# Sampled score maxima turned by VectorE in 32x32 blocks and stacked by 16 small DMAs a unit, in a 16-head attention layer

## The reference

```python
xn = _layernorm(x, axis=-1)
q = _split_heads(xn @ q_w.T + q_b, h) / scale        # k and v likewise
scores = jnp.einsum('bhqd,bhkd->bhqk', q, k)
attn = jax.nn.softmax(scores.astype(jnp.float32), axis=-1)
ctx = jnp.einsum('bhqk,bhkd->bhqd', attn, v)
x = x + (ctx @ out_w.T + out_b) + ffn(xn)             # ffn: fp8-rounded x and weight, 256 x 256
```

## Time and profile before

| what | us |
|---|---|
| median of 3 runs | 1987.59 (1986.44 to 1989.02) |
| the profiled execution, its own time | 1988.86 |
| its span (first to last instruction) | 1987.0 |
| PE busy | 1932.5 |
| ACT busy | 1827.5 |
| DVE busy | 1277.2 |

### The profile page before, as it was taken

How to read it: one execution, slowest core, us unless ns; L and a number is a source line. 1 busy time by engine, 2 the same in 40 slices (tenths; PEclk the granted TensorE clock), 3 DMA queues, 4 the chain that set the end, 5 groups by cost and what they waited for, 6 DMA issues and landing times.

```text
span 1987.0 us, 39086 instructions
## 1 busy us (share of the span) xinstructions
PE 1932.5 (97%) x13433; PEld 652.1 (33%) x13433; DVE 1277.2 (64%) x1789; ACT 1827.5 (92%) x2004; POOL 43.9 (2%) x53
## 2 busy tenths in 40 slices
PE   5969999999999999999999999999999999999988
PEld 3623333333333333333333333333333333333327
DVE  6645766656566766656566766656565766656556
ACT  2339999999999999999999999999999999999983
POOL 2000000000000000000000000000000000000000
PEclk9979999999999999999999999999999999999999
DMA  6870121203030121203030121202030121102022
GB/s 196 268 245 6 21 29 24 30 8 45 8 41 12 17 29 24 29 8 45 8 44 9 16 29 24 30 13 41 8 45 8 16 29 24 30 17 37 8 41 86
DMA packets 65524, 82.10 MB, mean 41 GB/s; under 512 B 9952, under 2 KB 47360, under 8 KB 62208
## 3 DMA queue, kind: packets, MB, share of 16 engines
q1 hardware_dynamic: 65472, 81.58, 20.3%
HBM read 54.79 MB, written 26.21 MB: 41 GB/s over the span
## 4 chain that ended last, share of the span: by engine, by line
PE 95%; DMA 2%; SPq 1%; DVE 1%; issue 1%; ACT 0%; ACTq 0%; DVEq 0%
PE banks L1086 48%; PE banks L1065 38%; PE banks L1092 3%; PE banks L976 2%; PE banks L1192 1%; PE banks L987 1%; DMA k_parts<-probs 1%; PE banks L1023 1%; PE banks L1043 0%; PE banks L1176 0%; PE banks L1183 0%; PE banks L960 0%; DMA q_st<-q_parts 0%; SPq L339 0%; DMA k_parts<-bits 0%
## 5 line engine op out<-in xcount | busy, mean ns | idle before, releaser
L583 ACT ACTIVATE probs<-banks 128x1024 f32<-128x1024 f32 x1923 | 1776.9, 1165 | 21.5 <-PE banks L1065 12.9
L1086 PE MATMUL banks<-probs,v_st 128*32 128x512 f32 x7680 | 1027.1, 607 | 2.9 <-DVE o_sb L800 2.9
L1065 PE MATMUL banks<-q_st,k_st 50*128 50x512 f32 x4102 | 833.2, 462 | 6.6 <-ACT probs L583 4.3
L1065 PEld LDWEIGHTS banks<-q_st,k_st 50*128 50x128 f32 x4102 | 373.7, 184 | 882.7 <-ACT probs L583 854.4
L834 DVE SCALAR_TENSOR_TENSOR d_probs<-d_probs,bits 128x1024 f32<-128x1024 f32 x256 | 313.7, 1225 | 8.8
L819 DVE TENSOR_SCALAR bits<-banks 128x512 int32<-128x512 f32 x256 | 177.2, 692 | 171.9 <-PE banks L1065 159.7
L1086 PEld LDWEIGHTS banks<-probs,v_st 128*32 128x32 f32 x7680 | 151.7, 108 | 305.3 <-issue 243.3
L800 DVE STREAM_TRANSPOSE o_sb<-banks 128x512 f32<-128x512 f32 x32 | 22.9, 717 | 299.7 <-PE banks L1086 299.7
L830 DVE SCALAR_TENSOR_TENSOR d_probs<-bits 128x1024 f32<-128x1024 f32 x128 | 156.9, 1226 | 7.3
L837 DVE SCALAR_TENSOR_TENSOR d_probs<-d_probs,powers 128x1024 f32<-128x1024 f32 x128 | 158.0, 1234 | 4.4
L825 DVE TENSOR_SCALAR bits<-bits 128x1024 int32<-128x1024 int32 x128 | 88.9, 695 | 4.4
(11 more groups left out here) (91 smaller groups left out, 482.9 us busy)
## 6 DMA issues: line engine op xcount, KB each, us to landing
k_st<-k_parts SPq DMA_DIRECT2D x204, 128.0 KB, 4.4
q_st<-q_parts SPq DMA_DIRECT2D x204, 64.0 KB, 5.0
q_parts<-probs SPq DMA_DIRECT2D x9, 512.0 KB, 6.1
k_parts<-probs SPq DMA_DIRECT2D x9, 512.0 KB, 6.2
xnT_copy<-probs SPq DMA_DIRECT2D x8, 512.0 KB, 4.4
probs<-xnT_copy SPq DMA_DIRECT2D x8, 512.0 KB, 6.7
w_f<-xnT_copy SPq DMA_DIRECT2D x16, 256.0 KB, 5.1
out_dram<-qt SPq DMA_DIRECT2D x16, 256.0 KB, 2.1
```

The costliest lines, as they stand in the source:

```text
L583: act.activation(probs[:, at:at + WIDE * CHUNK].rearrange("p (t c) -> p t c", t=WIDE), banks[:, bank:bank + WIDE, :], ACT.Exp, scale=1.0 / ...
L1065: return pe.matmul(out, k_mm[rows, kt * P:(kt + 1) * P], blocks[rows, qb // GROUPS], start=True, stop=True)
L1086: last = pe.matmul(banks[VCOLS * qb:VCOLS * (qb + 1), 6, :], v_st[:, kt, :], probs[:, at:at + CHUNK], start=first_one, stop=last_one, tile ...
```

## The change

The transposition on TensorE and its place in the order of jobs (slot 46; chunk 5 in the prologue) go, and with them the copy out of `misc` and the semaphore between VectorE and TensorE. VectorE makes the remainder part in rounded form, waits for it, and transposes `neg`, now 128x32, into `neg_row`, now 128x32 as well. Its transposition works on blocks of 32x32: row 32b + c of `neg_row` then holds column c of `neg` for the queries 32b to 32b + 31. A row of q's stack must therefore be put together from four blocks: `load_rows` issues 2 parts x 2 groups x 4 blocks = 16 DMAs a unit, each of 8 pieces of 32 values, in place of 4. The order of SyncE's queue stays. In the prologue VectorE does the whole at the start of chunk 5.

```diff
-    ROW_LOADS = 16 * GROUPS * PARTS
+    BLOCKS = P // (PARTS * UT)
+    ROW_LOADS = 16 * GROUPS * PARTS * BLOCKS
...
-        neg = sb("neg", [P, P // UT, UT])
+        neg = sb("neg", [P, PARTS, UT])
-        neg_row = sb("neg_row", [PARTS * UT, P])
+        neg_row = sb("neg_row", [P, PARTS * UT])
...
                 sp.wait_ge(c.row_ready, count)
                 for i in range(PARTS):
                     for g in range(GROUPS):
-                        at = g * GROUP + KROWS + i
-                        sp.dma_start(q_st[at:at + 1, u * UG:(u + 1) * UG].rearrange("o (t c) -> o t c", c=P),
-                                     neg_row[i * UT + g * GT:i * UT + (g + 1) * GT, :]).then_inc(c.row_in[u], 16)
+                        at, r0 = g * GROUP + KROWS + i, i * UT + g * GT
+                        to = q_st[at:at + 1, u * UG:(u + 1) * UG].rearrange("o (t b x) -> o b t x", t=GT, x=PARTS * UT)
+                        for b in range(BLOCKS):
+                            first_row = b * PARTS * UT + r0
+                            sp.dma_start(to[:, b], neg_row[first_row:first_row + GT, :]).then_inc(c.row_in[u], 16)
...
-                def minus_maxima(job, link0):
-                    negate(link0)
-                    to_rows(job)
...
-                    dve.tensor_tensor(neg[:, 1, :], neg_full[:, :], neg[:, 0, :], ALU.subtract).then_inc(c.neg_ready, 1)
-
-                def to_rows(job):
-                    dve.wait_ge(c.misc_full, job + 1)
-                    dve.tensor_copy(neg_row[:, :].bitcast(F32R), misc[0:PARTS * UT, 0:P]
-                                    ).then_inc(c.row_ready, 1)
-                    dve.wait_ge(c.row_ready, neg_count[0])
-                    dve.sem_inc(c.misc_free, 1)
+                    chain(dve.tensor_tensor(neg[:, 1, :].bitcast(F32R), neg_full[:, :], neg[:, 0, :], ALU.subtract),
+                          link0 + 3)
+                    dve.transpose(neg_row[:, :], neg[:, :, :].rearrange("p a t -> p (a t)")).then_inc(c.row_ready, 1)
...
-                def turn_maxima(job, count):
-                    misc_job(job, True)
-                    pe.wait_ge(c.neg_ready, count)
-                    pe.transpose(misc[:, 0:P], neg[:, :, :].rearrange("p a t -> p (a t)"), ident[:, :]).then_inc(c.misc_full, 1)
...
-                        if n == TURN_FIRST:
-                            turn_maxima(c.max_jobs, 1)
...
-                            jobs[u * UE + MAX_TURN] = (
-                                lambda u=u: turn_maxima(job_of[u] + (D_JOBS + c.max_jobs), h * 2 + (2 + u)))
```

More of the change, by code:

```diff
@@ L81, in program @@
     HALF = 2 * CHUNK
-    MAX_SLOTS, MAX_TURN = (36, 38), 46
+    MAX_SLOTS = (36, 38)
     UT4 = QB * len(A_ROWS)
@@ L224, in __init__ @@
                 self.misc_free = sem(f"{tag}_misc_free")
-                self.neg_ready = sem(f"{tag}_neg_ready")
                 self.row_ready = sem(f"{tag}_row_ready")
@@ L232, in __init__ @@
                 self.max_jobs = UT * (S // CHUNK) if full else 1
-                self.unit_jobs = QB * len(D_ROWS) + self.max_jobs + 1
+                self.unit_jobs = QB * len(D_ROWS) + self.max_jobs
                 self.head_jobs = UNITS * self.unit_jobs
@@ L746, in attend @@
             def attend(c):
-                MAX_LINKS = 2 + c.full * UT
+                MAX_LINKS = 3 + c.full * UT
                 SUM_LINKS = 2 if c.full else 3
@@ L769, in maxima @@
                         dve.wait_ge(c.misc_free, job0 + c.max_jobs)
-                    minus_maxima(job0 + c.max_jobs, link0)
+                    minus_maxima(link0)
                 def some_maxima(job):
@@ L776, in some_maxima, with minus_maxima @@
                                       ).then_inc(c.misc_free, 1)
-                def minus_maxima(job, link0):
-                    negate(link0)
-                    to_rows(job)
-                def negate(link0):
+                def minus_maxima(link0):
                     above = 0.0 if c.full else HEADROOM * UNIT
@@ L786, in negate @@
                     chain(dve.tensor_copy(neg[:, 0, :].bitcast(F32R), neg_full[:, :]), link0 + 2)
-                    dve.tensor_tensor(neg[:, 1, :], neg_full[:, :], neg[:, 0, :], ALU.subtract).then_inc(c.neg_ready, 1)
-                def to_rows(job):
-                    dve.wait_ge(c.misc_full, job + 1)
-                    dve.tensor_copy(neg_row[:, :].bitcast(F32R), misc[0:PARTS * UT, 0:P]
-                                    ).then_inc(c.row_ready, 1)
-                    dve.wait_ge(c.row_ready, neg_count[0])
-                    dve.sem_inc(c.misc_free, 1)
-                neg_count = [1]
+                    chain(dve.tensor_tensor(neg[:, 1, :].bitcast(F32R), neg_full[:, :], neg[:, 0, :], ALU.subtract),
+                          link0 + 3)
+                    dve.transpose(neg_row[:, :], neg[:, :, :].rearrange("p a t -> p (a t)")).then_inc(c.row_ready, 1)
                 def take_sums(h, u, link0):
@@ L855, in attend @@
                             dve.wait_ge(c.misc_free, c.max_jobs)
-                            negate(0)
+                            minus_maxima(0)
                         remainders(NCH + n, n % 2, 1, (0,))
-                        if n == TURN_FIRST:
-                            to_rows(c.max_jobs)
                         remainders(NCH + n, n % 2, 1, (1,))
@@ L874, in attend @@
                     maxima(0, 0)
-                JOB0 = c.max_jobs + 1
+                JOB0 = c.max_jobs
                 with dve.Fori(0, HEADS) as h:
@@ L878, in attend @@
                     lk = h * HEAD_LINKS + MAX_LINKS
-                    neg_count[0] = h * 2 + 2
                     for d in range(len(D_ROWS)):
@@ L889, in attend @@
                             d_exponentials(h, 1, d, half, job + (QB * d + 2 * half))
-                    neg_count[0] = h * 2 + 3
                     lk = lk + (MAX_LINKS + SUM_LINKS)
@@ L920, in _ @@
                 attend(second)
-                dve.wait_ge(second.misc_free, HEADS * second.head_jobs + second.max_jobs + 1)
+                dve.wait_ge(second.misc_free, HEADS * second.head_jobs + second.max_jobs)
                 dve.sem_inc(pass2_end, 1)
@@ L1098, in attend @@
                     all_max_jobs(0, 0, LOADS, True)
-                    pe.wait_ge(c.misc_free, c.max_jobs)
-                    turn_maxima(c.max_jobs, 1)
                 else:
@@ L1140, in maximum_first @@
                         all_max_jobs(u, j0, h * LOADS + LOADS * (1 + nxt))
-                        turn_maxima(j0 + c.max_jobs, h * 2 + (2 if u else 3))
                     for e in range(HE):
@@ L1157, in _ @@
             attend(first)
-            pe.wait_ge(first.misc_free, HEADS * first.head_jobs + first.max_jobs + 1)
+            pe.wait_ge(first.misc_free, HEADS * first.head_jobs + first.max_jobs)
             pe.wait_ge(flag_ok, 1)
@@ L1164, in _ @@
                 attend(second)
-                pe.wait_ge(second.misc_free, HEADS * second.head_jobs + second.max_jobs + 1)
+                pe.wait_ge(second.misc_free, HEADS * second.head_jobs + second.max_jobs)
                 pe.sem_inc(pass2_end, 1)
```

## The result

The changed kernel takes 1997.28 us, the median of 12 executions (1991.57 to 2006.69); the kernel before, run beside it, 1987.08 (12 executions, 1980.33 to 1990.22). The medians are 10.2 us apart. The ratio is 1.0055, 95% interval 1.0038 to 1.0071: 10.9 us slower, between 7.6 and 14.1. That is above the 0.2% that can be told; the time is inside the range and 4.5 us above the forecast of 1992.8. The profiled execution took 1998.2 us with a span of 1996.4, against 1988.86 and 1987.0: 9.4 us more span.

A forecast was written before the change was run, and what follows sets the result against it. ScalarE's exponentials were taken to set the time. Loop 0, first unit +5.2 us and end 0 took the profiled 1988.86 us to 1994.1 and the median 1987.59 to 1992.8; range 1988.5 to 2003.0.

The forecast's parts named there:

- The sign: Whole kernel: slower, chance 0.68; same 0.24; faster 0.08.
- the start: Prologue: the first exponential starts at 140.15 instead of 134.92, +5.2 us.
- the queue: SyncE: sixteen row DMAs of 0.68 us take 10.9 us, and all rows are there at 921.05.
- the loop: Main loop: ScalarE's units stay 55.75 us apart, so the change costs 0 there.
- I cost the removal at 0: Loop: taking out TensorE's transposition, 0.45 us of TensorE time a unit, gains nothing, hidden by score tiles ScalarE has in hand.
- rival D: TensorE is the bound: 14.9 us faster, 1972.7; if only the 6.2 us of gaps went, 1981.4; chance 0.08.
- VectorE: Its 128x32 transposition takes 0.25 us; rows are ready at 909.2 instead of 912.44, 3.2 us earlier.
- ScalarE feels a delay above 1.05 us: Loop: late rows cost ScalarE time only beyond 1.05 us of delay, a landing after 921.65.
- margin of 0.6 us: Loop: distance from the rows' forecast landing at 921.05 to the limit of 921.65.
- The first unit: Row DMAs end at 132.2, the awaited save lands at 139.9, the first exponential starts at 140.15: +5.2 us.
- B: Rival: rows late in every unit, beyond 0.72 us between DMA starts; 1999.9 at 0.735, 2044 at 0.83; chance 0.20.
- C: Rival: the extra issue time disappears at the start too; 0 to 3 us, 1987.6 to 1990.5; chance 0.12.

The follow-up runs named there:

- half the DMAs: Changed kernel with only the rounded part's eight row DMAs sent, remainder rows left zero by two more memsets: 1987.52 us, ratio 1.0009 to the kernel before.
- slot 50: Kernel before with the TensorE transposition in slot 50 instead of 46, nothing else: 1984.42 us, ratio 0.9990.
- eight and eight with GpSimd: Changed kernel with eight of a unit's sixteen row DMAs issued by GpSimd, eight by SyncE: 1982.87 us, ratio 0.9989 to the kernel before.
- all sixteen on GpSimd: Changed kernel with all sixteen row DMAs of a unit issued by GpSimd, none by SyncE: 1985.12 us, ratio 0.9987 to the kernel before.
- seventeen DMAs: Changed kernel with one more small DMA, into a spare tile, ahead of the sixteen: 2049.74 us (one execution).
- eighteen: Changed kernel with two more small DMAs, into a spare tile, ahead of the sixteen: 2096.48 us, ratio 1.0549 to the kernel before.
- the first unit by GpSimd: Changed kernel with only the first unit's sixteen row DMAs issued by GpSimd: 1997.68 and 1996.65 us, ratios 1.0065 and 1.0061 to the kernel before.

## Why the prediction came out as it did

The sign, the start and the queue were right; the loop was not. The loop's 6.7 us stood in the sum as 0, so the change cost twice the +5.2 that I had forecast. That the total still lies in the range, 4.5 us from the forecast, is luck: no step of the sum kept the loop's error small beside the range.

**What the change removes: "I cost the removal at 0" failed.** The argument was that ScalarE has no gap in the 55.54 us after 910.26. It rested on 0.926 us as the pace of an exponential, and that was the mean over a block with small losses in it. At 0.90 us the transposition shows as 0.14, and the runs put it at 0.11 us a unit (55.75 to 55.64, in three ways: half the DMAs, slot 50, GpSimd): a gain of 3.4 us, not 14.9 or 6.2 (rival D) and not 0.

**VectorE: right.** 0.21 us against 0.25, and the first row DMA starts 1.06 us before ScalarE's block (412.90 - 411.84), as forecast (910.26 - 909.2).

**SyncE's queue: right, its end a little late.** 10.87 us for sixteen, forecast 10.9. The sixteenth starts at 411.84 + 15 x 0.68 = 422.04, and the scores start at 423.87, 1.83 us later, weight load included, where I had 1.65 to the landing (the profile doesn't list the landing of SyncE's row DMAs). TensorE waits 0.62 us in this unit and 0.70 in the mean instead of 0.45; its scores start 10.97 us after ScalarE's block, 10.34 before the change: 0.63 late.

**"ScalarE feels a delay above 1.05 us": this step failed most.** I counted the exponentials in hand at the waiting scores and took them as the reserve. But TensorE doesn't go on with scores: behind the late ones stands a weighted sum of 1.06 us, and only then the scores of the next two slots. These started 11.76 us after ScalarE's block before (922.02 - 910.26) and 12.39 after (425.29 - 412.90), late by the same 0.63. Their exponential started 1.05 us behind them before (923.07, in the single starts) and needs 0.55, as 425.83 - 425.29 again shows. The reserve is 0.50 us. With the 0.14 by which ScalarE now is earlier, the loss is 0.63 - 0.50 + 0.14 = 0.27, and 0.26 is measured. So the limit lay at 0.50, not at 1.05, and my "margin of 0.6 us" was spent already. In the neighbouring unit the scores are 0.74 late (479.79 - 468.71 = 11.08 instead of 10.34); the same sum gives 0.38 there, and 0.36 is measured in that place. The further 0.12 four exponentials on I haven't worked out. Measured against the 55.64 of a unit with neither cost, late rows cost 0.33 us in the mean, 10.2 us, less the 3.4 of the transposition: the 6.7 that the loop grew. Half the DMAs, and eight and eight with GpSimd, take away the 10.2 and nothing else of the loop; all sixteen on GpSimd take away 7.8.

**The first unit: right, mis-sized by a tenth.** +4.6 us for +5.2. The issue took the 11.1 us foreseen; too large was the term behind it, from its end to the first exponential: 7.95 us in the sum (3.8 + 3 x 1.31 + the release), 7.3 measured (130.78 to 138.09). The profile gave 3.2 in absolute time, since chunk 4 was earlier. The kernel before with only this part slower by 0.35% shows that it counts.

**The rivals.** B's mechanism, late rows in every unit, is what happened, at a spacing of 0.68 us at which B wasn't to begin: its condition (0.72) was worked out from the wrong reserve. I gave it 0.20. C was wrong in the trace by 4.6 us against its 0 to 3. What the Trainium skill says in DMA: Bandwidth & Descriptors, § Issuing engines are not separate DMA queues, that the sequencer's time is usually small beside the DMA, does not hold for this run of sixteen: 10.87 us of issue, then 1.83 to the scores. Its 2.0 us of fixed time (§ Anatomy of one DMA) lies as far above those 1.83 us as my 1.65 lies below. The page gives it for DMAs issued by GpSimd, and for GpSimd's row DMAs the traces here show less, 1.6 us in the median from issue to landing.

**Sum by what was measured:** +6.7 (loop) + 4.6 (start) - 0.5 (end) = +10.8; the ratio gives +10.9, the medians +10.2.

## What to carry to other kernels

The reserve of the bounding engine is not read at the instruction that waits but at the one that is late next: follow the waiting engine's program past the wait, to its next delivery, and count from there. A long unbroken block of a busy engine proves nothing about tenths of a microsecond; take its pace from two neighbouring single starts, and what the block takes beyond that is lost somewhere in it. When small DMAs replace big ones, their count times the issue time is a latency on one queue: start them as early as the data allows, or split them over two queues, and look at what else waits in that queue.

## What the runs showed of the hardware that I had not expected

**A wait of 1.3 us or more can cost TensorE its clock.** In the units of the kernel after, with waits of 0.6 to 1.3 us, it stays at 1.00. With seventeen DMAs (1.27 to 1.66 us) it falls to 0.50 in 16 of 31 units, with eighteen (1.96 to 2.11 us) in 30, and with waits of 3.8 to 4.0 us in all, for 3.4 or 6.8 us each. One DMA more than sixteen therefore cost some 50 us and two 100, where their issue alone is worth 21 and 42 (0.68 us, 31 units).

**The start's half clock differs between executions.** The stretch at 0.50 ended at 154.0 in the profile before and at 156.8 after (windows of the kernel after, columns as above):

```profile
140.00:145.00 5.00, 4.92 (x19) 1.52 (x23) 3.81 (x7) 4.28 (x6) 0.00 (x0) 0.50 0.04 11
150.00:155.00 5.00, 5.00 (x23) 1.28 (x23) 4.77 (x5) 3.11 (x4) 0.00 (x0) 0.50 0.00 0
155.00:160.00 5.00, 5.00 (x36) 1.42 (x29) 0.37 (x1) 3.93 (x5) 0.00 (x0) 0.82 0.00 0
```

It was 10 to 27 us long in the traces of this case, and in it ScalarE stands still 1.5 us for every two exponentials. In the kernels before and after it ended some 19 us behind the first exponential, and the 53 exponentials from there took 56.2 and 56.0 us; in the traces of half the DMAs and of the first unit by GpSimd it ended 6 to 10 us behind it, and they took 50.3 to 52.1. The times of the kernel before follow: over 79 executions, those with a mean granted clock of 0.993 have a median of 1981.2 us (16), those with 0.990 one of 1987.4 (42). That is half of the spread of one kernel (1979.2 to 1991.0), and as much as the effects measured here.

**GpSimd issues a small DMA faster than SyncE,** 0.53 against 0.68 us each, and its rows take 1.6 us (median) from issue to landing.
